# Batch 0's keys and queries projected twice side by side and written in place by the engines, batch 1 prepared between the first heads

## The chip, the cores and the metric

One Trainium2 chip, one of its cores. The metric is the device time of one execution in microseconds (us). The kernel before took 519.92, 517.23 and 517.09 us in three runs; the median is 517.23 us.

TensorE (PE) multiplies, VectorE (DVE) and ScalarE (ACT) read its results out of PSUM, GpSimd (POOL) works on SBUF alone, and SyncE (SP) issues the DMAs. Each runs its own list of instructions in order and waits on semaphores.

## The reference, cut to what matters

Two layers over x (4 batches of 256 tokens, width 128) and a context (4 batches of 512 rows, width 96). The change touches the attention of layer 0; what follows it is only told in words.

```python
B, S, _ = x.shape            # after a layer norm of x;  4, 256
scale = DIM_HEAD ** (-0.5)   # 8 heads of 64
q = (x @ Wq).reshape(B, S, HEADS, DIM_HEAD).transpose(0, 2, 1, 3)
k = (context @ Wk).reshape(B, L, HEADS, DIM_HEAD).transpose(0, 2, 1, 3)
v = (context @ Wv).reshape(B, L, HEADS, DIM_HEAD).transpose(0, 2, 1, 3)
attn = jnp.einsum('bhsd,bhld->bhsl', q, k) * scale
attn = jax.nn.softmax(attn, axis=-1)
out = jnp.einsum('bhsl,bhld->bhsd', attn, v)
return out @ Wo + bo
```

Then come layer 0's feed-forward part (fixed-point rounding and a piecewise linear GELU), layer 1's attention (16 heads of 8), a small feed-forward part and a mixture of 8 experts, two per token.

## The kernel before, in words

Everything runs from one list of steps, `order`, that `schedule()` builds: each step has a kind and indices, as ("k0", 1, 3), and each engine walks the list and does its part of every step that it knows. So the list sets the order of work on every engine. Iteration `it` of the list is one batch of one layer (0 to 3 layer 0, 4 to 7 layer 1); a step stands at a place counted in heads of that iteration, from the table PLACES, or from SHIFTED where that names the iteration. Iteration it computes scores and outputs of its batch and, between the heads, prepares the next.

Layer 0 keeps keys and queries as 16-bit high and low parts, so that a score is a sum of products over a stacked axis. For a head, kA holds the high part of the key twice (64 rows each), qA the high part of the query over its low part, kB the low part of the key, qB the high part of the query; rows 64 to 67 of kB and qB carry a selector and the row maxima, which a score subtracts. Projections, transposes and maxima all pass through four PSUM banks, the ring p_misc. For a projection TensorE takes a bank (`misc_take`), ScalarE writes the high part, and VectorE writes the difference, which frees it.

- `keys0` ("k0", b, m): two heads at once, 128 rows (L423); ScalarE copies to kx (L1004), VectorE takes the difference (L748). `queries0` ("q0", b, i): likewise (L447, L1023, L753), into qx.
- `stack0` ("stack0", b): kx and qx have two heads over each other and must be sorted into kA, kB, qA and qB. SyncE does so with 12 DMAs (L1247 to L1249), six for the keys once all four key steps are done, then six for the queries.
- `maxima` ("max", 0, b, h): scores of tokens by keys for the row maxima (L464, reduced at L759); for h = 0 it waits for all 12 DMAs. `rows`: the maxima of four heads are transposed and copied into qB (L773).
- `scores` ("sc", 0, b, h): L491, then the exponential on ScalarE (L1042). GpSimd sums each head's four tiles ("sum", L1181 to L1183), and `attend` ("av", L510) multiplies with the values; its fourth chunk ends with the sums' product (L517), which waits for GpSimd, and the sums of the next four heads wait for it.
- `init`: memsets on VectorE (L764, L765) and GpSimd; ("init", 4) is a block on GpSimd that prepares layer 1's kS (L1155 to L1165). "ln", "xn", "xT": layer norm; its square root comes from GpSimd (L1139, L1140), in GpSimd's order.

Of the kernel before, what the change touches and what calls it, by code (L numbers as in the profile page):

```python
# [5 lines left out]
ALU = mybir.AluOpType  # L6
# [5 lines left out]
P = 128  # L12
# [23 lines left out]
    0: {"max": (1.5, 1.0), "sum": 1.38, "av": (-0.38, 0.96), "f_ln": -0.65, "f_xn": 0.92, "f_xT": 1.2,  # L36
        "up0": (1.4, 0.13), "round": 1.57, "floor": 2.0, "nodes": 2.17, "slope": 3.0, "interp": 3.5, "ident": 3.7,
# [3 lines left out]
        "zeros": 3.67, "init": (1.0, 2.0), "rows": 0.84},  # L41
    1: {"max": (2.4, 1.01), "av": (0.3, 1.0), "f_ln": 0.18, "f_xn": 1.29, "f_xT": 1.39, "up0": (1.87, 0.4),
        "round": 2.76, "floor": 2.8, "nodes": 3.39, "slope": 4.4, "interp": 5.2, "ident": 5.69, "down0": 5.86,
        "q1_ln": 8.4, "q1_xn": 9.17, "q1_xT": 10.0, "q1": 11, "k1": 9.53, "bounce": 11.61, "sT": 4.1,
        "oT": (4.64, 2.0), "aT": (6.0, 2.0), "y0": (7.3, 2.0), "oT1": (4.52, 0.7), "aT1": 6.54, "h1": 8.28,
        "y1": 9.07, "v1": 5.94, "stage": (0.62, 1.9), "split": (0.6, 1.9), "ex_ln": (11.14, 1.0),
        "ex_xn": (12.57, 1.0), "ex_xT": (12.68, 1.0), "logits": (14.14, 1.0), "route": 16.14, "rows": 2.43},
# [17 lines left out]
def schedule():  # L65
# [18 lines left out]
    for what in first:  # L84
        put(-1, 0, *what)
    for n, h in enumerate(range(4, H0)):
        put(0, 0.5 + 0.6 * n, "max", 0, 0, h)
    put(0, 3.1, "rows", 0, 0, 1)
    put(0, 0.1, "k0", 1, 3)
    for i in range(2):  # L90
        put(0, 0.7 + 0.6 * i, "q0", 1, i)
# [1252 lines left out]
```

## Time and profile before

| what | us |
|---|---|
| median of three runs (all: 517.09, 517.23, 519.92) | 517.23 |
| span of the profiled execution (its own time outside the span isn't given) | 515.0 |
| TensorE busy in the span | 440.4 |
| VectorE busy | 367.9 |
| ScalarE busy | 266.9 |
| GpSimd busy | 175.6 |

The span begins with the first instruction that the profiler records, and the times of all views are counted from there. A busy TensorE is one with a matmul in flight; at which of its two clocks it ran is told by the granted clock, 1.00 for 2.4 GHz and 0.50 for 1.2 GHz. In front of an instruction stands how long its engine had been idle, and what ended that; "issue" means that the profile shows nothing it waited for, which is how a wait for a DMA can look.

### The profile page before, as it was taken

The page shows a single profiled execution, that of the slowest core. Times are in us where ns is not written, and L with a number is a line of the kernel's source. Part 1 is how long each engine was busy: PE and PEld are TensorE (multiplying, and loading weights), DVE is VectorE, ACT ScalarE, POOL GpSimd, SP SyncE. Part 2 cuts the span into 40 slices and gives each one's busy share as a digit, 9 for nine tenths or more (in the row PEclk, how much of TensorE's full clock was granted, in tenths as well). Part 3 has the DMA queues.
Part 4 walks back from the last instruction along what each step waited for, and adds up shares of the span by engine and source line. Part 5 has one row for each costly group of instructions (what it writes and reads, how often), then busy time and mean ns, then how long its engine had stood idle before and what let it go on. Part 6 is the DMA issues. An engine that isn't in the chain of part 4 may idle for free.

```text
span 515.0 us, 8942 instructions
## 1 busy us (share of the span) xinstructions
PE 440.4 (86%) x3344; PEld 250.5 (49%) x3344; DVE 367.9 (71%) x718; ACT 266.9 (52%) x504; POOL 175.6 (34%) x205
## 2 busy tenths in 40 slices
PE   8569698995779868969975995999989999999996
PEld 4225354563356445535432542544536665656565
DVE  5665374654875798879958994794368787987875
ACT  4415244642725632475656363668765555554653
POOL 4307954634554572750516041630130004000000
PEclk9867798997899988997997898999999999999999
DMA  5755316017004006331262027210000000000000
GB/s 160 170 122 116 67 28 158 1 27 158 22 1 57 1 1 154 57 91 33 73 84 84 2 73 87 83 42 2 2 1 1 1 2 0 2 22 2 1 1 22
DMA packets 33023, 25.91 MB, mean 50 GB/s; under 512 B 4589, under 2 KB 30381, under 8 KB 32877
## 3 DMA queue, kind: packets, MB, share of 16 engines
q1 hardware_dynamic: 32981, 25.35, 22.2%
q8 instruction: 27, 0.44, 0.4%
q14 instruction: 15, 0.12, 0.1%
HBM read 12.10 MB, written 2.10 MB: 28 GB/s over the span
## 4 chain that ended last, share of the span: by engine, by line
PE 57%; DVE 22%; ACT 7%; issue 7%; DMA 3%; SPq 2%; POOL 1%; DVEq 0%; POOLq 0%; ACTq 0%
PE p_o L663 7%; PE p_misc L646 7%; PE p_sc L491 6%; PE p_sc L646 6%; DVE mx L759 6%; PE p_misc L464 6%; PE p_o L523 4%; PE p_o L510 4%; PE p_misc L397 4%; DVE xn L722 3%; PE p_misc L423 3%; DVE probs L946 2%; DMA region<-kx 2%; PE p_misc L555 2%; ACT probs L1108 2%
## 5 line engine op out<-in xcount | busy, mean ns | idle before, releaser
L759 DVE TENSOR_REDUCE mx<-p_misc 128x1 f32<-128x512 f32 x192 | 122.4, 684 | 41.9 <-PE p_misc L464 40.3
L1042 ACT ACTIVATE probs<-p_sc 128x512 f32<-128x512 f32 x192 | 104.5, 596 | 65.9 <-PE p_sc L491 65.6
L1108 ACT ACTIVATE probs<-p_misc 128x512 f32<-128x512 f32 x64 | 38.1, 597 | 56.6 <-PE p_sc L646 56.6
L946 DVE TENSOR_TENSOR probs<-probs,p_sc 128x512 f32<-128x512 f32 x64 | 44.0, 687 | 26.5 <-ACT probs L1108 24.6
L464 PE MATMUL p_misc<-kS,qS 96*128 96x512 f16 x128 | 41.9, 404 | 16.7 <-issue 8.5
L646 PE MATMUL p_misc<-qS,region 128*128 128x512 f16 x192 | 52.1, 380 | 3.8 <-DVE probs L946 2.6
L646 PE MATMUL p_sc<-qS,region 128*128 128x512 f16 x192 | 51.9, 379 | 0.0
L1181 POOL TENSOR_TENSOR psums<-probs 128x256 f32<-128x256 f32 x32 | 26.0, 811 | 61.5 <-PE p_o L517 58.0
L663 PEld LDWEIGHTS p_o<-region,probs 128*128 128x128 f16 x720 | 42.7, 98 | 7.1
L663 PE MATMUL p_o<-region,probs 128*128 128x128 f16 x720 | 45.1, 219 | 0.0
L1139 POOL TENSOR_SCALAR veps<-meanvar 128x2 f32<-128x2 f32 x16 | 3.5, 218 | 121.7 <-DVE meanvar L711 121.2
L491 PE MATMUL p_sc<-qS,kS 128*128 128x256 f16 x256 | 41.3, 282 | 4.1 <-ACT probs L1042 3.8
L510 PE MATMUL p_o<-probs,v 128*64 128x256 f32 x256 | 38.2, 423 | 7.1 <-ACT probs L1042 7.1
L951 DVE TENSOR_TENSOR probs<-probs 128x512 f16<-128x512 f32 x64 | 43.8, 684 | 0.0
L523 PE MATMUL p_o<-probs,v 128*32 128x256 f32 x512 | 41.5, 402 | 0.0
L1115 ACT CAST probs<-probs 128x512 f16<-128x512 f32 x64 | 39.1, 611 | 1.4 <-DVE probs L946 1.4
L491 PE MATMUL p_sc<-region 128*128 128x256 f16 x256 | 35.8, 286 | 0.9 <-DVE region L773 0.9
L491 PEld LDWEIGHTS p_sc<-qS,kS 128*128 128x128 f16 x256 | 23.6, 99 | 19.8 <-ACT probs L1042 7.9
L464 PE MATMUL p_misc<-region 128*128 128x512 f16 x64 | 22.0, 426 | 12.7 <-issue 12.5
L491 PEld LDWEIGHTS p_sc<-region 128*128 128x128 f16 x256 | 25.5, 102 | 12.3 <-issue 3.7
L1199 POOL TENSOR_TENSOR region<-v,region 128x512 f16<-128x512 f32 x24 | 29.3, 1222 | 1.9
L646 PEld LDWEIGHTS p_sc<-qS,region 128*128 128x128 f16 x192 | 18.8, 98 | 22.6
(163 smaller groups left out, 678.5 us busy)
## 6 DMA issues: line engine op xcount, KB each, us to landing
region<-kx SPq DMA_DIRECT2D x24, 256.0 KB
v<-in_L_ffn_W_dram SPq DMA_DIRECT2D x24, 256.0 KB, 2.8
region<-qx SPq DMA_DIRECT2D x24, 128.0 KB
kS<-kS SPq DMA_DIRECT2D x1, 1664.0 KB
kS<-k_scratch SPq DMA_DIRECT2D x12, 128.0 KB
k_scratch<-kx SPq DMA_DIRECT2D x4, 256.0 KB, 3.1
qS<-q_scratch SPq DMA_DIRECT2D x12, 64.0 KB
probs<-in_ctx_dram SPq DMA_DIRECT2D x1, 576.0 KB, 6.0
```

What stands on the lines that cost most here:

```text
L464: pe.matmul(ps, q[:, i * P:(i + 1) * P], k, start=True, stop=True).then_inc(full, 1)
L491: last = pe.matmul(p_sc[:, half, j * S:(j + 1) * S], k[:, kt * P:(kt + 1) * P], q, start=(i == 0), stop=(i == len(pairs) - 1))
L510: pe.matmul(p_o[64 * i:64 * i + 64, 0, m * S:(m + 1) * S], v0[:, b % 2, kt, h * DH0:(h + 1) * DH0], probs[:, h % 8, kt * S:(kt + 1) * S], ...
L523: last = pe.matmul(p_o[32 * j:32 * j + 32, n % 2, 0:S], v1[:, b % 2, c, h * VW:h * VW + 32], probs[:, h % 8, c * S:(c + 1) * S], start=(c ...
L646: last = pe.matmul(ps[:, f % 2, :], w[:, ws, e, f * P:(f + 1) * P], xh[:, xs, half * C:(half + 1) * C], start=(i == 0), stop=(i == 2))
L663: last = pe.matmul(p_o[:, n % 2, i * P:(i + 1) * P], hh[:, n % 2, hs, f, i * P:(i + 1) * P], ew[2][:, ws, e, f * P:(f + 1) * P], start=(at ...
L759: dve.tensor_reduce(mx[:, b % 2, i, h:h + 1], ps, AX_X, ALU.max).then_inc(free, 1)
L946: dve.tensor_tensor(hp[:, k % 2, :], sg[:, k % 2, :], p_sc[:, k % 2, :], ALU.mult).then_inc(hp_done, 1)
L951: dve.tensor_tensor(hh[:, n % 2, 1, f, :], hp[:, k % 2, :], hh[:, n % 2, 0, f, :], ALU.subtract).then_inc(hl_done, 1)
L1042: act.activation(probs[:, h % 8, half * 512:(half + 1) * 512], p_sc[:, half, :], ACT.Exp, scale=(DH0 if layer == 0 else DH1) ** -0.5).then ...
L1108: act.activation(sg[:, k % 2, :], p_misc[:, k % 2, :], ACT.Silu).then_inc(sg_done, 1)
L1115: act.copy(hh[:, last_n % 2, 0, last_f, :], hp[:, (k - 1) % 2, :]).then_inc(hh_done, 1)
```

## The change

Batch 0 no longer passes through kx, qx and DMAs. `keys0_twice` projects one head into both halves of the 128 output rows, as two matmuls of 64 columns of weights side by side; ScalarE writes both halves straight into kA, VectorE writes the difference into kB. `queries0_twice` does the same for two heads: ScalarE writes the high part twice into qA, VectorE replaces the lower half by the difference, and GpSimd copies the upper half into qB. So batch 0 has eight key steps and four query steps in place of four and two. The product over kB and qB now reads 68 rows instead of 128, so only four rows of kB are zeroed and none of qB. Batch 0's twelve DMAs go. The first list ends after four heads' maxima; what remained of batch 0 and all of batch 1's preparation (context, values, keys, queries, norms) stand between the first heads of iteration 0. The 15 loads of later weights stand before the DMAs of batch 1. All places were chosen anew, those of the later iterations too.

```diff
-    0: {"max": (1.5, 1.0), "sum": 1.38, "av": (-0.38, 0.96), "f_ln": -0.65, "f_xn": 0.92, "f_xT": 1.2,
...
+    0: {"max": (1.5, 1.0), "sum": 1.38, "av": (-0.38, 0.96), "f_ln": -1.31, "f_xn": 0.76, "f_xT": 1.2,
...
 SHIFTED = {
...
-    first = [("init", 0), ("warm", 10), ("ln", "q0", 0), ("split_w", 0), ("cT", 0), ("warm", 6), ("xn", "q0", 0), ("k0", 0, 0), ("warm", 4), ("xT", "q0", 0), ("k0", 0, 1), ("k0", 0, 2), ("k0", 0, 3),
-             ("q0", 0, 0), ("q0", 0, 1), ("stack0", 0), ("split_w", 1), ("cT", 1), ("ln", "q0", 1), ("v0", 0, 0), ("v0", 0, 1), ("xn", "q0", 1), ("init", 1),
-             ("v0", 0, 2), ("v0", 0, 3), ("cT", 2), ("cT", 3), ("xT", "q0", 1),
-             ("max", 0, 0, 0), ("k0", 1, 0), ("max", 0, 0, 1), ("k0", 1, 1), ("max", 0, 0, 2), ("k0", 1, 2), ("max", 0, 0, 3), ("rows", 0, 0, 0)]
+    first = [("zero", 0), ("warm", 10), ("ln", "q0", 0), ("split_w", 0), ("cT", 0), ("warm", 6), ("init", 0), ("xn", "q0", 0), ("k0h", 0), ("xT", "q0", 0), ("k0h", 1),
+             ("q0h", 0), ("k0h", 2), ("max", 0, 0, 0), ("k0h", 3), ("q0h", 1), ("max", 0, 0, 1), ("max", 0, 0, 2), ("k0h", 4), ("max", 0, 0, 3), ("k0h", 5), ("q0h", 2), ("rows", 0, 0, 0)]
...
+            put(it, place["q0b"][0] + place["q0b"][1] + 0.01 if it == 0 else -0.01, "stack0" if nxt[0] == 0 else "stack1", nxt[1])
...
+            def keys0_twice(h):
+
+                if h == 0:
+                    pe.wait_ge(wc_split, 1)
+                    misc_done(pe, ("cT", 0))
+                ps, full = misc_take(pe, ("k0h", h))
+                for i, (ws, cs) in enumerate(((0, 0), (1, 0), (0, 1))):
+                    for rows in (slice(0, DH0), slice(DH0, P)):
+                        last = pe.matmul(ps[rows, :], wc[:, ws, h * DH0:(h + 1) * DH0], cT[:, cs, 0:C], start=(i == 0), stop=(i == 2))
+                last.then_inc(full, 1)
+
+            def queries0_twice(i):
...
+                ps, full = misc_take(pe, ("q0h", i))
+                for j in range(2):
+                    h = 2 * i + j
+                    for rows in (slice(0, DH0), slice(DH0, P)):
+                        last = pe.matmul(ps[rows, j * S:(j + 1) * S], wq0[:, h * DH0:(h + 1) * DH0], xT[:, 0, :], start=True, stop=True)
+                last.then_inc(full, 1)
...
+                if layer == b == 0:
+                    pe.wait_ge(k_first, h + 1)
+                    misc_done(pe, ("q0h", h // 2))
...
-                    pairs = [(kA[:, b % 2, h, :], qA[:, b % 2, h, :]), (kB[:, b % 2, h, :], qB[:, b % 2, h, :])]
+                    if b == 0:
+                        misc_done(pe, ("k0h", h))
+                        pe.wait_ge(q_second, h // 2 + 1)
+                    pairs = [(kA[:, b % 2, h, :], qA[:, b % 2, h, :]), (kB[0:SEL0 + 4, b % 2, h, :], qB[0:SEL0 + 4, b % 2, h, :])]
...
+            def keys0_twice(h):
+                dve.wait_ge(k_first, h + 1)
+                ps, free = misc_wait(dve, ("k0h", h))
+                dve.tensor_tensor(kB[0:DH0, 0, h, :], ps[0:DH0, :], kA[0:DH0, 0, h, :], ALU.subtract).then_inc(free, 1)
...
-                if b and m == 0:
-                    act.wait_ge(k_stacked, 96 * b)
+                if b >= 2 and m == 0:
+                    act.wait_ge(k_stacked, 96 * (b - 1))
...
+                act.copy(kA[:, 0, h, :], ps).then_inc(k_first, 1)
...
+                pool.tensor_copy(qB[0:DH0, 0, high, :].rearrange("p h n -> p (h n)"),
+                                 qA[0:DH0, 0, high, :].rearrange("p h n -> p (h n)")).then_inc(q_second, 1)
```

**TensorE, the first projections up to batch 0's first maxima.** L423 is the key projection, L447 the queries, L431 the values, L397 transposes (of context rows where they read probs, of tokens where they read xn), L464 the maxima; in the changed kernel L488 and L499 are the doubled projections, L453 the transposes and L541 the maxima. Before:

```order
L423 MATMUL p_misc<-cT,wc 128x512 x3
L414 MATMUL p_o<-qx 128x512 x4
L397 MATMUL p_misc<-ident,xn 128x128 x2
L423 MATMUL p_misc<-cT,wc 128x512 x9
L447 MATMUL p_misc<-xT,wq 128x256 x4
L397 MATMUL p_misc<-ident,probs 96x128 x4
L431 MATMUL p_misc<-wc,cT 128x512 x12
L397 MATMUL p_misc<-ident,probs 96x128 x8
L397 MATMUL p_misc<-ident,xn 128x128 x2
L464 MATMUL p_misc<-region 128x512 x2
```

And in the changed kernel:

```order
L488 MATMUL p_misc<-cT,wc 64x512 x6
L453 MATMUL p_misc<-ident,xn 128x128 x2
L488 MATMUL p_misc<-cT,wc 64x512 x6
L499 MATMUL p_misc<-xT,wq 64x256 x4
L488 MATMUL p_misc<-cT,wc 64x512 x6
L541 MATMUL p_misc<-region 128x512 x2
L488 MATMUL p_misc<-cT,wc 64x512 x6
L499 MATMUL p_misc<-xT,wq 64x256 x4
L541 MATMUL p_misc<-region 128x512 x4
```

The first maxima stand behind three doubled key steps and one query step, and the values and the other context transposes have moved behind them.

**TensorE, from batch 1's last projections (where its DMAs are issued) to its first maxima.** L491 and L571 are the scores, L510 and L590 the products with the values, L477 and L521 the single projections in the changed kernel; the last row of each piece is ("max", 0, 1, 0), which waits for the DMAs. Before:

```order
L447 MATMUL p_misc<-xT,wq 128x256 x2
L464 MATMUL p_misc<-region 128x512 x2
L491 MATMUL p_sc<-region 128x256 x8
L464 MATMUL p_misc<-region 128x512 x2
L491 MATMUL p_sc<-region 128x256 x8
L397 MATMUL p_misc<-ident,mx 4x128 x2
L423 MATMUL p_misc<-cT,wc 128x512 x3
L510 MATMUL p_o<-probs,v 64x256 x4
L464 MATMUL p_misc<-region 128x512 x2
```

And in the changed kernel:

```order
L521 MATMUL p_misc<-xT,wq 128x256 x2
L571 MATMUL p_sc<-region 128x256 x8
L541 MATMUL p_misc<-region 128x512 x2
L477 MATMUL p_misc<-cT,wc 128x512 x6
L571 MATMUL p_sc<-region 128x256 x8
L453 MATMUL p_misc<-ident,mx 4x128 x2
L477 MATMUL p_misc<-cT,wc 128x512 x6
L590 MATMUL p_o<-probs,v 64x256 x4
L541 MATMUL p_misc<-region 128x512 x2
```

All four key steps of batch 2 now stand ahead of batch 1's first maxima, where one did.

**GpSimd, the block for kS among batch 0's sums.** L1181 to L1183 and L1285 to L1287 are one head's sum, L1158 to L1162 with the four selections L1145 (in the changed kernel L1255 to L1259 and L1242) are the block, L1236 and L1237 are ("ln", "q0", 3). Before, from the fourth head's sum:

```order
L1181 TENSOR_TENSOR psums<-probs 128x256
L1182 TENSOR_TENSOR psums<-psums,probs 128x256
L1183 TENSOR_TENSOR psums<-psums,probs 128x256
L1158 MEMSET tri 128x64
L1159 AFFINE_SELECT tri<-tri 128x64
L1162 MEMSET kS 128x4096
L1145 AFFINE_SELECT kS<-kS 32x2048 x4
L1181 TENSOR_TENSOR psums<-probs 128x256
```

In the changed kernel, from the sixth head's sum:

```order
L1285 TENSOR_TENSOR psums<-probs 128x256
L1286 TENSOR_TENSOR psums<-psums,probs 128x256
L1287 TENSOR_TENSOR psums<-psums,probs 128x256
L1255 MEMSET tri 128x64
L1256 AFFINE_SELECT tri<-tri 128x64
L1259 MEMSET kS 128x4096
L1242 AFFINE_SELECT kS<-kS 32x2048 x4
L1285 TENSOR_TENSOR psums<-probs 128x256
L1286 TENSOR_TENSOR psums<-psums,probs 128x256
L1287 TENSOR_TENSOR psums<-psums,probs 128x256
L1236 TENSOR_SCALAR veps<-meanvar 128x2
L1237 TENSOR_TENSOR rstd<-veps,mhalf 128x2
```

The block has moved behind two more sums: from ahead of the fifth head's sum to between the sixth's and the seventh's, and ahead of batch 3's norm.

## Rows read from the trace of the kernel before

**Rows 1.** The page's first part: busy us, share of the span, instructions.

```profile
PE 440.4 (86%) x3344; PEld 250.5 (49%) x3344; DVE 367.9 (71%) x718; ACT 266.9 (52%) x504; POOL 175.6 (34%) x205
```

**Rows 2.** TensorE's waits: us in total, times, longest.

```profile
PE p_misc L464 <- issue: 21.0, 5, 6.2
```

**Rows 3.** The chain of waits: start us, us, what.

```profile
52.87 3.68 issue
```

**Rows 4.** Groups of instructions, VectorE, 0 to 57 us: busy us, mean ns, idle.

```profile
L759 DVE TENSOR_REDUCE mx<-p_misc 128x1 f32<-128x512 f32 x16 | 10.2, 682 | 4.2 <-PE p_misc L464 4.2
L748 DVE TENSOR_TENSOR kx<-p_misc,kx 128x512 f16<-128x512 f32 x9 | 6.1, 691 | 8.1 <-ACT kx L1004 8.1
L764 DVE MEMSET region<- 64x2048 f32 x2 | 3.5, 1765 | 1.0 <-issue 1.0
```

**Rows 5.** Timeline to 40 us: start us, us, engine, line; in brackets the idle before.

```profile
8.03 0.81 PE L423 MATMUL p_misc<-cT,wc 96*128 96x512 f16 x3 [0.17 <-DVE cT L743]
...
13.55 0.73 SPq L1247 DMA_DIRECT2D region<-kx  x1
...
16.23 4.45 PE L431 MATMUL p_misc<-wc,cT 96*128 96x512 f16 x12 [1.96 <-DVE wc L737]
...
27.53 1.01 PE L464 MATMUL p_misc<-region 128*128 128x512 f16 x2 [5.75 <-issue]
...
38.08 1.89 PE L491 MATMUL p_sc<-region 128*128 128x256 f16 x8 [0.91 <-DVE region L773]
```

**Rows 6.** Windows, 18 to 20 us: busy by engine, granted clock, DMA.

```profile
18.00:20.00 2.00, 2.00 (x6) 0.68 (x5) 0.77 (x3) 0.71 (x2) 0.64 (x1) 0.50 0.91 210
```

**Rows 7.** Timeline, 42 to 57 us: batch 1's DMAs, batch 2's first key copy, the maxima.

```profile
42.74 0.60 SPq L1247 DMA_DIRECT2D region<-kx  x1
...
52.89 0.58 ACT L1004 CAST kx<-p_misc 128x512 f16<-128x512 f32 x1 [2.08 <-DMA region<-kx]
...
56.55 1.01 PE L464 MATMUL p_misc<-region 128*128 128x512 f16 x2 [4.53 <-issue]
```

**Rows 8.** Timeline, TensorE, 74 to 77 us: products side by side between whole ones.

```profile
74.37 0.81 PE L431 MATMUL p_misc<-wc,cT 96*128 96x512 f16 x3
75.11 1.08 PE L510 MATMUL p_o<-probs,v 128*64 128x256 f32 x8
76.13 0.60 PE L464 MATMUL p_misc<-region 128*128 128x512 f16 x2
```

**Rows 9.** Timeline, 55 to 84 us: GpSimd's block, sums and norm, and who follows.

```profile
55.68 3.51 POOL L1162 MEMSET kS<- 128x4096 f32 x1
...
59.34 8.14 POOL L1145 TENSOR_SCALAR_AFFINE_SELECT kS<-kS 32x2048 f16<-32x2048 f16 x4
...
72.37 0.73 POOL L1181 TENSOR_TENSOR psums<-probs 128x256 f32<-128x256 f32 x1 [4.90 <-PE p_o L517]
...
79.92 0.71 POOL L1140 TENSOR_TENSOR rstd<-veps,mhalf 128x2 f32<-128x2 f32 x1
...
81.75 1.43 DVE L722 TENSOR_SCALAR xn<-x_sb,meanvar,rstd 128x128 f32<-128x128 f32 x2
...
83.24 0.44 PE L397 MATMUL p_misc<-ident,xn 128*128 128x128 f32 x2 [1.21 <-DVE xn L722]
```

**Rows 10.** Timeline, 112 to 130 us: batch 3's DMAs, its first maxima, a feed-forward product.

```profile
112.78 0.59 SPq L1247 DMA_DIRECT2D region<-kx  x1
...
126.59 1.01 PE L464 MATMUL p_misc<-region 128*128 128x512 f16 x2 [2.24 <-issue]
...
127.39 1.91 PE L555 MATMUL p_misc<-xT,f0w 128*128 128x256 f32 x4
```

**Rows 11.** Timeline, TensorE, three later waits for maxima of layer 1.

```profile
228.86 0.39 PE L464 MATMUL p_misc<-kS,qS 96*128 96x512 f16 x1 [2.10 <-DVE rden L778]
...
270.06 0.59 PE L464 MATMUL p_misc<-kS,qS 96*128 96x512 f16 x2 [2.23 <-issue]
...
277.98 0.61 PE L464 MATMUL p_misc<-kS,qS 96*128 96x512 f16 x1 [4.24 <-DVE mx L759]
```

More of the change, by code:

```diff
@@ new lines @@
+    (2, 'f_ln'): -0.22, (2, 'floor'): 2.08, (2, 'init'): (1.75, 1.58), (2, 'initb'): 1.47, (2, 'interp'): 3.48,
+    (2, 'k0b'): (2.05, 0.4), (2, 'k0h'): (0.36, 0.4), (2, 'lnb'): -1.95, (2, 'max0'): (0.32, 0.78),
+    (2, 'q0'): (2.15, 0.82), (2, 'q0_ln'): 0.21, (2, 'q0b'): (1.9, 0.38), (2, 'q1'): 5.66, (2, 'q1_ln'): 4.48,
+    (2, 'round'): 1.68, (2, 'rows'): 1.95, (2, 'slope'): 2.73, (2, 'sum'): 2.36, (2, 'v0'): (3.6, 1.02),
+    (2, 'v0a'): (0.56, 0.25), (2, 'v1'): 5.51, (2, 'xTb'): 0.97, (2, 'xnb'): 0.36, (2, 'zeros'): 3.55,
@@ L681, in down_last @@
                     last.then_inc(y_full, 1)
-            steps = {"dn_last": down_last, "warm": warm, "cT": context, "k0": keys0, "v0": values0, "xT": xt, "q0": queries0, "max": maxima, "rows": rows, "sc": scores,
+            steps = {"dn_last": down_last, "warm": warm, "cT": context, "k0": keys0, "k0h": keys0_twice, "q0h": queries0_twice, "v0": values0, "xT": xt, "q0": queries0, "max": maxima, "rows": rows, "sc": scores,
                      "av": attend, "sT": sums_t, "oT": heads_t, "aT": heads_back, "y0": project0, "up0": up0, "down0": down0,
@@ L974, in _ @@
             dve.memset(warm_in.bitcast(F32), 0.0).then_inc(warm_set, 1)
-            steps = {"split_w": split_w, "cT": context, "ln": norm, "xn": normed, "xT": xt, "k0": keys0, "q0": queries0, "init": init, "max": maxima, "rows": rows, "sT": sums_t, "oT": heads_t,
+            steps = {"split_w": split_w, "cT": context, "ln": norm, "xn": normed, "xT": xt, "k0": keys0, "k0h": keys0_twice, "q0h": queries0_twice, "q0": queries0, "zero": zero, "max": maxima, "rows": rows, "sT": sums_t, "oT": heads_t,
                      "y0": project0, "round": rounded, "floor": floor, "slope": slope, "interp": interp, "ident": identity, "down0": add0,
@@ L1115, in activate @@
                     act.copy(hh[:, last_n % 2, 0, last_f, :], hp[:, (k - 1) % 2, :]).then_inc(hh_done, 1)
-            steps = {"split_w": split_w, "cT": context, "k0": keys0, "v0": values0, "xT": xt, "q0": queries0, "rows": rows, "sc": softmax, "av": outputs,
+            steps = {"split_w": split_w, "cT": context, "k0": keys0, "k0h": keys0_twice, "q0h": queries0_twice, "v0": values0, "xT": xt, "q0": queries0, "rows": rows, "sc": softmax, "av": outputs,
                      "aT": heads_back, "up0": up0, "nodes": nodes_at, "k1": keys1, "q1": queries1, "aT1": heads_back1, "h1": up1,
@@ L1211, in _ @@
             pool.sem_inc(const_pe, 1)
-            steps = {"ln": norm, "sum": sums, "init": init, "route": route, "split": split}
+            steps = {"ln": norm, "q0h": queries0_twice, "sum": sums, "init": init, "route": route, "split": split}
             for kind, *at in order:
```

132 lines of the change are left out of this document (89 added, 43 removed), and 32 rows, old and new, of tables (PLACES, SHIFTED).

## The prediction

> **What bounds the kernel now.** The page's first part comes first: TensorE is busy 440.4 of 515.0 us, VectorE 367.9 [rows 1]. No engine is full, so the question is where TensorE stands still. Its waits answer: five times it stood at maxima with nothing in the profile to wait for, 21.0 us in all [rows 2]. These are the first maxima of a batch, and what they wait for are DMAs: the first needed 13.98 us from the first DMA (13.55) to the maxima (27.53), with TensorE idle for 5.75 [rows 5], the second 13.81 (42.74 to 56.55) with 4.53 idle [rows 7], and the chain of waits has that wait on the path [rows 3]. After each such stop TensorE works at half clock: two maxima take 1.01 us at 56.55 [rows 7] and 0.60 at 76.13 [rows 8]. The change takes away the first of these stops and rearranges what surrounds the second. The reader should see that the first score stands at 38.08 [rows 5], but that batch 1's maxima, 18.5 us later, are the next gate, and that they hang on when batch 1's DMAs begin, not on when batch 0 begins.
>
> All times below are of the profiled execution (span 515.0); the median of the runs, 517.23, lies 2.2 above it, and I subtract my sum from the median.
>
> **Step 1, batch 0's first score.** The doubled key step starts where the single one does, 8.03 [rows 5]. Two products side by side cost little more than one: the block at 75.11 holds eight 64-column halves, and the next instruction starts 1.02 later [rows 8], where one after the other they would take 1.7. So I take 0.75 for a doubled key step (a single one 0.64, 0.81 with its tail) and 1.0 for a doubled query step. Following the steps through TensorE, ScalarE (0.58 a copy) and VectorE (0.69), the first doubled query is done at 12.65 and the fourth pair of maxima at 21.1; the maxima's transpose, its two copies and the waits between bring the first score to 23, 15 us earlier than before.
>
> **Step 2, the start of batch 1's DMAs.** They need the last of batch 1's key steps. What VectorE must do from 12.65 until then, by the list: 6 doubled keys, 3 doubled queries, 4 keys and 1 query, 3 context parts, all at 0.69 (17 of them, 11.7), 7 pairs of maxima at 1.28 (eight took 10.2; 9.0), one memset of 1.76 [rows 4], and 3.5 of small ones, an estimate. That is 25.9, so 38.5 if it never waits. My walk has it wait 1.7 more, where a doubled query or a softmax pair stands ahead of it on ScalarE: **40.3**. Before, it was 42.74 [rows 7]. Here the gain of step 1 goes: batch 0's preparation was overlapped with DMA waits, and now values, contexts and batch 1's keys follow after the first score. The zeroing of qB (one memset of about half L764's time per batch) is gone, and four more keys and two more queries cost VectorE 4.1; both are in the count. Bounds: 38.5, and 50 if TensorE ran at half clock throughout (its work in this stretch is some 25 us at full clock).
>
> **Step 3, batch 1's first maxima.** The keys land 10.15 after the first DMA (52.89 less 42.74), and ScalarE's copy of batch 2's first key waits for just that [rows 7]. In the new order this copy stands in front of the fourth head's softmax, and the fourth key step and the first value products in front of the maxima. So: 40.3 + 10.15, two copies, a softmax pair of 1.1 (as two copies), then value products at half clock, 2.0: the maxima start at 55.1, not 56.55. The queries' DMAs have landed by 54.1 and no longer end the wait. Three key steps of batch 2 are behind us that were ahead before.
>
> **Step 4, GpSimd's block.** From here TensorE needs some 7.9 us to the sums' product of the first four heads (three chunks of values, two scores, three maxima pairs, part of it at half clock): 63.0, where before it ended at 72.17, 0.2 before the sum at 72.37 that waited for it [rows 9]. GpSimd's order now decides. Three heads' sums and the norm's root take 8.26 (72.37 to 80.63); before, they were all that followed. Now the block for kS stands among them, 3.51 + 8.14 [rows 9] and an estimated 0.45 for the small triangle ahead of them, 12.1. The root is ready at 63.0 + 0.2 + 8.26 + 12.1 = 83.6, the normalised tokens 1.43 later, and TensorE's transpose of batch 3's tokens starts at **85.1**, before it was 83.24 [rows 9]. TensorE would be there at about 78, so some 7 us of the lead are waited away: +1.9 in place of a gain. Behind it one value step (1.29 at half clock, twice its 0.64) is already done, and value products now cover the copy of the transposed tokens (an estimated 0.46): +0.2 is left.
>
> **Step 5, batch 3.** Its DMAs start after the last score of batch 1, and 13.81 later the maxima follow (112.78 to 126.59) [rows 10]. One value step moves behind that score: -0.65. Two steps that stood behind the maxima, a product of the feed-forward part at 1.91 [rows 10] and the transposed maxima, now fall into the wait: -1.9 for TensorE; VectorE's rounding, which ends the next chain, gains less, and I take -1.0.
>
> **Step 6, the later places.** A maxima pair now stands before batch 3's reciprocals on VectorE, and another before the slope; these two waits of TensorE were 2.10 and 4.24 [rows 11]. I take half of them, 3.2, since the work put behind is due as well. Against it one feed-forward product moves out of the wait at 270.06 [rows 11]: +1.0. Together -2.2; bounds -6.3 (both waits gone) and +2.2 (neither, and something else late).
>
> **At nothing:** the 15 weight loads, which now run before 20 us (nobody waits for them before layer 0's output); GpSimd's four copies of query halves (it is idle there; if they took 2 us each they would still be ahead of the first scores); the narrower product over 68 rows; the first clearing of kB. The layer 1 reordering from 325 us on: neither side is worth a sign.
>
> **Sum:** +0.2 - 0.65 - 1.0 - 2.2 = -3.65, so 517.23 - 3.65 = **513.6**.
>
> **A rule of the skill against the trace.** The value products side by side start at 75.11, before the full-width ones in front of them have ended (75.18), and the full-width ones behind start at 76.13, before their end (76.19) [rows 8]: no time is lost at the change of shape. The Trainium skill (TensorEngine Tiling (Array Packing), Tiling Modes, Key Properties) says that changing the tiling mode drains TensorE. The trace speaks against that as a cost here. By that rule the head would have some 18 changes at 0.17, half of them on the path, and the sum would be 515.1, an estimate.
>
> **The rivals.**
> - *The lead is kept (0.18).* GpSimd's block does not stand in the way, because the sums' product comes earlier than I have it or the tokens are needed later. The lead at that product is 9.2, less 2.9 for the six steps now behind it; 6.3 less some waiting at batch 2's maxima, 6, takes the place of +0.2: 517.2 - 6 - 0.65 - 1.0 - 2.2 = 507.4. For it: the order is new everywhere. Against: the block's place between two sums is plain in the list.
> - *Slower: TensorE's clock falls in the head (0.14).* After 1.96 us without work the granted clock went to 0.50 [rows 5, 6]. From 12 to 40 us TensorE is now busy three quarters, in pieces of 0.4 to 1.0 with gaps up to 1.3. At half clock the doubled steps take 1.5 and 2.0 and TensorE sets the pace instead of VectorE. The place is the stretch before batch 1's DMAs; each us of delay there goes on to the end. If they start at 46.5 rather than 40.3 and step 6 gives nothing: 517.2 + 6.4 - 0.65 - 0.5 = 522.5. It decides from a start at 44 on, where the other gains are used up.
> - *Not side by side (0.07).* If the halves ran one after the other, or each change of shape drained the array (0.17, the tail of 0.81 over 0.64 at 8.03, at 18 changes: 3.1), TensorE would have 3 to 7 us more in the head, half of it on the path: about 517.
> - *The late places give nothing (0.20).* 515.8 to 517.5.
> - *The forecast (0.41)*, 511 to 516; I give 0.19 of it to below 512.1.
>
> **The numbers.** Predicted 513.6. The range takes in the first rival and, of the slower one, all but its end: 506 to 521.5. One per cent, 5.2 us, is about what a measurement of this kernel can tell from no change: faster by more than that 0.18 + 0.19 = 0.37, slower 0.15 (the second rival and a little of the others), within 0.48.
>
> **What the new profile would show.** Step 1: the first score near 23. Step 2: first DMA from kx near 40, with VectorE almost gapless before it; a start after 44 with a granted clock of 0.50 is the slower rival. Step 3: batch 1's first maxima near 55, behind value products. Step 4: POOL's kS memset starting near 68, and TensorE idle some 7 us at a transpose of tokens near 85; if that idle time is missing, the first rival holds. Step 5: a feed-forward product inside the wait before batch 3's maxima. Step 6: the waits of 2.10 and 4.24 halved. I am wrong if the head's 15 us arrive at batch 2's scores at all, or if a new wait stands in layer 1, where I have looked at order only.

## The result

| | before | changed |
|---|---|---|
| median of the runs, us | 517.27 (4 runs, 517.09 to 519.92) | 526.21 (4 runs, 525.68 to 526.77) |
| ratio, 95% interval | | 1.0146 [1.011, 1.0181] |
| the same, measured again (the last experiment) | 519.02 (11 runs) | 526.24 (6 runs), 1.0122 [1.0078, 1.0166] |
| profiled execution, span | 515.0 | 524.2 (its time 526.16) |
| mean granted TensorE clock | 0.934 | 0.922 |

The change makes the kernel 7 to 9 us slower. The forecast was 513.6 with a range of 506 to 521.5, and 0.15 for slower.

On the page of the changed kernel TensorE answers to [rows 1] with 11.2 us more of busy time, for 56 matmuls more. The four windows further down hold 11.2 us of it with nearly the same count of matmuls, so there it works slower, not more.

```profile
PE 451.6 (86%) x3400; PEld 256.1 (49%) x3400; DVE 373.5 (71%) x722; ACT 269.4 (51%) x510; POOL 178.9 (34%) x209
```

TensorE's waits (us in total, times, longest) answer to [rows 2]. The waits of the maxima for DMAs ("issue") fell from 21.0 to 7.7. Two single waits took their place: 7.8 for VectorE's part of a key of batch 2, which itself waits for a DMA, and 8.0 for normalised tokens.

```profile
PE p_misc L453 <- DVE xn L802: 16.0, 7, 8.0
PE p_misc L477 <- DVE kx L828: 7.8, 1, 7.8
PE p_misc L541 <- issue: 7.7, 3, 5.5
```

**The head.** The timeline of the changed kernel, against [rows 5, 7] (start us, us, engine, line; in brackets the idle time before): a doubled key step, the first score, the first DMA of batch 1, ScalarE's copies of batch 2's keys, which wait for it, batch 2's last key step, batch 1's first maxima, and the first four heads' sums' product.

```profile
7.98 0.84 PE L488 MATMUL p_misc<-cT,wc 96*64 96x512 f16 x6 [0.38 <-DVE cT L823]
...
23.79 0.39 PE L571 MATMUL p_sc<-region 128*128 128x256 f16 x2
...
40.73 0.73 SPq L1351 DMA_DIRECT2D region<-kx  x1
...
50.95 1.07 ACT L1093 CAST kx<-p_misc 128x512 f16<-128x512 f32 x2 [9.18 <-DMA region<-kx]
...
52.31 1.46 PE L477 MATMUL p_misc<-cT,wc 96*128 96x512 f16 x3 [7.77 <-DVE kx L828]
...
55.61 1.03 PE L541 MATMUL p_misc<-region 128*128 128x512 f16 x2
...
63.20 0.64 PE L597 MATMUL p_o<-psums,ones 128*32 128x256 f32 x8
```

The first score is 14.3 us earlier, the DMAs 2.0, the maxima 0.9. The product is 8.3 earlier (it started at 71.5 in the kernel before). Then comes GpSimd, against [rows 9]: its block for kS, the root for batch 3's tokens, the tokens on VectorE, and TensorE's transpose.

```profile
69.51 3.51 POOL L1259 MEMSET kS<- 128x4096 f32 x1
...
73.17 8.08 POOL L1242 TENSOR_SCALAR_AFFINE_SELECT kS<-kS 32x2048 f16<-32x2048 f16 x4
...
84.20 0.71 POOL L1237 TENSOR_TENSOR rstd<-veps,mhalf 128x2 f32<-128x2 f32 x1
...
85.01 1.59 DVE L802 TENSOR_SCALAR xn<-x_sb,meanvar,rstd 128x128 f32<-128x128 f32 x2 [5.54 <-POOL rstd L1237]
...
86.65 0.69 PE L453 MATMUL p_misc<-ident,xn 128*128 128x128 f32 x2 [7.96 <-DVE xn L802]
```

The whole lead is gone here: the sums' product of the second four heads (the second group) starts at 93.6, before it was 92.4.

**Behind the head** 1.2 us of lateness become 8.9 by 366 us (the same transpose of tokens stands at 366.8 and at 375.7), and stay. Windows between the same products of both kernels (stretch, length, then busy time by engine, and third from last the granted clock), first before:

```profile
133.60:159.70 26.10, 19.68 (x141) 12.44 (x143) 20.48 (x34) 12.53 (x21) 13.46 (x14) 0.93 0.08 21
159.70:205.70 46.00, 38.01 (x260) 23.16 (x258) 36.96 (x66) 21.19 (x38) 25.60 (x31) 0.93 0.28 53
205.70:251.30 45.60, 38.98 (x290) 22.42 (x288) 39.34 (x72) 25.17 (x47) 22.66 (x29) 0.93 0.24 57
251.30:301.80 50.50, 39.07 (x301) 19.89 (x300) 41.57 (x74) 28.50 (x56) 17.61 (x20) 0.90 0.28 57
```

and the changed kernel:

```profile
134.90:164.10 29.20, 22.48 (x139) 14.73 (x138) 19.12 (x32) 12.79 (x21) 13.44 (x14) 0.82 0.06 19
164.10:211.00 46.90, 40.52 (x260) 24.81 (x258) 38.26 (x67) 20.94 (x38) 26.06 (x31) 0.85 0.26 52
211.00:258.40 47.40, 40.18 (x299) 23.00 (x298) 41.04 (x73) 26.05 (x49) 22.98 (x28) 0.93 0.20 51
258.40:311.50 53.10, 43.76 (x300) 22.29 (x300) 42.31 (x75) 28.99 (x57) 17.42 (x20) 0.84 0.27 60
```

The four together are 8.4 us longer. In three of them (6.6 of the 8.4) TensorE's busy time grew by 2.5 to 4.7 us with nearly the same count of matmuls, and the granted clock fell from 0.93 or 0.90 to 0.82 to 0.85. In the third window, 1.8 us longer, the clock is the same, and a wait of 2.10 us has become 3.46 (shown further down).

### The profile page after: what moved, and what is told of

It reads as the page before. It is cut to its first block, busy times and chain, and to the rows that moved or that the text cites. A ratio compares the mean times of both kernels' runs of the same rounds, so it can differ in the third digit from the quotient of the medians.

```text
span 524.2 us, 9069 instructions
## 1 busy us (share of the span) xinstructions
PE 451.6 (86%) x3400; PEld 256.1 (49%) x3400; DVE 373.5 (71%) x722; ACT 269.4 (51%) x510; POOL 178.9 (34%) x209
## 4 chain that ended last, share of the span: by engine, by line
PE 58%; DVE 21%; ACT 5%; issue 5%; POOL 5%; DMA 3%; SPq 1%; POOLq 0%; DVEq 0%; ACTq 0%
PE p_o L743 7%; PE p_sc L571 7%; PE p_misc L726 6%; PE p_sc L726 6%; PE p_misc L541 6%; PE p_o L590 5%; PE p_o L603 5%; DVE mx L851 4%; PE p_misc L453 4%; PE p_misc L645 2%; DVE xn L802 2%; DVE probs L1035 2%; PE p_misc L635 2%; ACT probs L1205 2%; POOL kS L1242 1%
## 5 line engine op out<-in xcount | busy, mean ns | idle before, releaser
L541 PE MATMUL p_misc<-kS,qS 96*128 96x512 f16 x128 | 42.6, 410 | 16.8 <-DVE mx L851 7.7
L1285 POOL TENSOR_TENSOR psums<-probs 128x256 f32<-128x256 f32 x32 | 25.7, 803 | 63.6 <-PE p_o L597 57.1
L590 PE MATMUL p_o<-probs,v 128*64 128x256 f32 x256 | 39.7, 437 | 6.7 <-ACT probs L1139 6.7
L571 PE MATMUL p_sc<-qS,kS 128*128 128x256 f16 x256 | 42.7, 288 | 1.4 <-ACT probs L1139 0.9
L1236 POOL TENSOR_SCALAR veps<-meanvar 128x2 f32<-128x2 f32 x16 | 4.0, 249 | 114.8 <-DVE meanvar L791 114.6
L571 PE MATMUL p_sc<-region 128*128 128x256 f16 (+1 forms) x256 | 36.2, 286 | 0.0
L571 PEld LDWEIGHTS p_sc<-qS,kS 128*128 128x128 f16 x256 | 23.6, 103 | 20.2 <-issue 7.0
L571 PEld LDWEIGHTS p_sc<-region 128*128 128x128 f16 (+1 forms) x256 | 25.9, 103 | 11.5 <-issue 3.1
L1302 POOL CAST region<-v 128x512 f16<-128x512 f32 x24 | 16.6, 691 | 42.0 <-DMA v<-in_L_ffn_W_dram 41.4
```

The lines of the kernel that those rows point to most:

```text
L541: pe.matmul(ps, q[:, i * P:(i + 1) * P], k, start=True, stop=True).then_inc(full, 1)
L571: last = pe.matmul(p_sc[:, half, j * S:(j + 1) * S], k[:, kt * P:(kt + 1) * P], q, start=(i == 0), stop=(i == len(pairs) - 1))
L590: pe.matmul(p_o[64 * i:64 * i + 64, 0, m * S:(m + 1) * S], v0[:, b % 2, kt, h * DH0:(h + 1) * DH0], probs[:, h % 8, kt * S:(kt + 1) * S], ...
```

## The experiments

All ratios are to the kernel before, run beside them on the same chip, with 95% intervals. One execution of a kernel differs from the next by up to 0.9% either way in these runs, so a difference below some 0.5% between two experiments is not resolved.

**Which part costs?** Two theories: the later places cost the time themselves (A), or the head does (B). Four runs. In the first, the entries of the two tables of places for iterations 2 to 7 are those of the kernel before, for instance

```diff
-    (3, 'k1'): -0.05, (3, 'sT'): 4.74, (4, 'y1'): 6.03, ...
+    (3, 'k1'): 2.03, (3, 'sT'): 3.68, (4, 'y1'): 9.07, ...
```

> The changed kernel, with the places of the kernel before for the third to eighth batch (iterations 2 to 7); the doubled projections, the first list and the places of iterations 0 and 1 stay as changed. Theory A (the later places cost the time, 8 us by the table of starts: the second group's sums' product is only 1.2 us late at 93.6, everything after that is growth): 517 to 519 us, the first query transpose still 3 us late with its wait of 8 us. Theory B (the head's lateness sets in what phase the later batches run, and the clock falls with it, whatever the later places are): 524 to 527 us.

Measured: 1.0034 [0.9998, 1.007], 520.57 us. That lies in neither range, nearer to A: 0.9% (4.6 us) of the second measurement of the changed kernel, 1.0122, are gone. The wait of 8.0 us at 87 is still there.

The second moves GpSimd's kS block (and with it, by one sum, a clearing of qS of 1.80 us; every other engine's list stays):

```diff
-    (0, 'init'): (2.99, 1.87),
+    (0, 'init'): (2.99, 1.22),
```

> The changed kernel with one edit: GpSimd's clearing and filling of kS (12.6 us) stands before the sums of heads 4 and 5 instead of behind them, so that it runs where GpSimd idles from 57.4 to 64.1 us. Both theories: the wait of 8 us for the normalised queries at 86.65 goes, since the block ends near 70 and the rstd is computed near 76 and no longer at 84.2; the second group's sums' product starts near 86 and no longer at 93.6. Theory A: that lead is kept in part, 518 to 523 us, the growth of the later batches stays. Theory B: the growth goes with it, 512 to 517 us. If the lead is lost at the next transfer instead, 525 to 527 us.

Measured: 0.9953 [0.9922, 0.9983], 515.88 us. Its trace, where the block begins in GpSimd's idle time (it ends some 4 us after the next sum could have begun) and the root comes 7.7 us earlier:

```profile
56.93 3.51 POOL L1259 MEMSET kS<- 128x4096 f32 x1
60.58 8.08 POOL L1242 TENSOR_SCALAR_AFFINE_SELECT kS<-kS 32x2048 f16<-32x2048 f16 x4
...
76.49 0.71 POOL L1237 TENSOR_TENSOR rstd<-veps,mhalf 128x2 f32<-128x2 f32 x1
...
80.66 0.44 PE L453 MATMUL p_misc<-ident,xn 128*128 128x128 f32 x2 [0.71 <-DVE xn L802]
```

The second group's product starts at 86.7, 6.9 us earlier than in the changed kernel, and the two traces are 7 to 10 us apart everywhere behind it. One number in a table takes 1.7% (8.8 us) off, and makes the change faster than the kernel before. The time is in B's range, but the other half of B, that the growth behind the head goes with its lateness, is not what the trace shows: the four windows take 29.1, 46.9, 47.4 and 52.2 us at clocks of 0.82, 0.85, 0.93 and 0.84, as in the changed kernel, and the lead over the kernel before, 5.7 us at this product, is used up by the end of the span (515.7 against 515.0; the profiled execution was the slowest of its 12).

The third is the kernel before with the changed later places:

> The kernel before, with the changed kernel's places for iterations 2 to 7 and nothing else of the change. Theory A (the later places cost the time themselves): 522 to 526 us. Theory B: 516 to 518.5 us.

Measured: 1.0009 [0.9976, 1.0042], 519.29 us, just above B's range. A falls in its plain form: beside the old head no cost of these places is resolved.

The fourth is the first one for iterations 4 to 7 alone, and a fifth, sent later, does iterations 2 and 3 alone:

> The changed kernel with the places of the kernel before for iterations 4 to 7 alone. In the changed kernel the lateness is 5.3 us by 205 us and 9 us by 366 us. Theory A: the share of the places from iteration 4 on, some 3.5 us, goes: 521.5 to 523.5 us. Theory B: 524 to 527 us.

> The changed kernel with the places of the kernel before for iterations 2 and 3 alone. With those of 4 to 7 it was 1.0126 of the kernel before, with all of 2 to 7 1.0034, and as it stands 1.0122. If the loss of the later places lies in iterations 2 and 3 (the order around down0, where the clock stays low longer): 1.003 to 1.006, 521 to 522 us. If each half alone does nothing and only both together do: 1.010 to 1.014.

Measured: 1.0126 [1.0074, 1.0178], 524.96 us, and 1.0097 [1.0061, 1.0133], 523.43 us. Neither half gives back what both do (1.0034).

The traces tell more of the later places than the times do. Us from the second sums' product to the fourth (that of 133.6 before and 134.9 changed), and from the fourth to the end:

| trace | second to fourth | fourth to end |
|---|---|---|
| kernel before | 41.2 | 381.4 |
| the same with the changed later places | 38.9 | 385.9 |
| changed kernel | 41.4 | 389.3 |
| the same with the old later places | 42.5 | 381.9 |
| changed kernel, block early | 40.1 | 389.0 |
| the same with the old later places (below) | 43.2 | 385.0 |

Beside each of the three heads the changed later places give 1.1 to 3.2 us in the first stretch and take 4.0 to 7.4 in the second. Each row is one execution, comparable to 2 or 3 us only (last section), so the signs are better shown than the sizes.

**The block's place by itself.** The kernel before, with GpSimd's block where the change has it. Two clearings of qS (1.80 us each) move by two sums with it; the lists of all other engines do the same work in the same order:

```diff
-    (0, 'init'): (0.81, 2.0),
+    (0, 'init'): (2.99, 1.87),
```

> The kernel before with GpSimd's kS block at the changed kernel's place, behind the sums of heads 4 and 5, and nothing else; every other engine's list is the same. If the block's place is what costs the changed kernel its time: the block starts near 77 and ends near 90 and no longer at 67.5, the query transpose of 83.2 waits for it until near 94, and the time is 525 to 529 us. If it matters only beside the new head or later places: 517 to 520 us.

Measured: 1.0209 [1.0172, 1.0246], 529.97 us, 1 us above the first case. The transpose of [rows 9], which waited 1.21 us at 83.24:

```profile
93.07 0.69 PE L397 MATMUL p_misc<-ident,xn 128*128 128x128 f32 x2 [12.88 <-DVE xn L722]
```

This edit alone makes the kernel before slower than the changed one.

**Only the root behind the block?** The changed kernel, its block where it was, with batch 3's statistics and root ahead of it:

```diff
-            step("q0_ln", "ln", "q0", b + 2)
+            put(0, 4.3, "ln", "q0", 3) if it == 1 else step("q0_ln", "ln", "q0", b + 2)
```

> The changed kernel with this one edit: the statistics and rstd of batch 3's queries ahead of the sums of head 3; the kS block stays behind the sums of heads 4 and 5. If what costs the time is only the rstd that queues behind the block on GpSimd: the wait of 8.0 us at 86.7 goes though the block stands where it did, and the time is that of the block moved early, 515 to 519 us. If the block costs it otherwise too (the sums of heads 6 and 7 behind it, which the product at 93.6 reads, end at 88.9): 519 to 522 us.

Measured: 0.9985 [0.9945, 1.0026], 519.39 us, some 1.4% less than the changed kernel and at the lower end of the second case. The wait is halved, not gone. GpSimd's select, VectorE's copy of maxima and tokens, and the transpose:

```profile
73.44 8.09 POOL L1242 TENSOR_SCALAR_AFFINE_SELECT kS<-kS 32x2048 f16<-32x2048 f16 x4
```

```profile
77.60 2.15 DVE L862 COPY region<-mrow 4x1024 f16<-4x1024 f16 x1 [1.08 <-ACT mrow L1077]
79.79 2.07 DVE L802 TENSOR_SCALAR xn<-x_sb,meanvar,rstd 128x128 f32<-128x128 f32 x2
```

```profile
81.92 0.69 PE L453 MATMUL p_misc<-ident,xn 128*128 128x128 f32 x2 [3.91 <-DVE xn L802]
```

The root is no longer late. VectorE's two instructions are slow beside the select: 2.15 and 2.07 us, where the kernel before needs 0.72 and 1.43 beside GpSimd's sums, so the block costs some 2 us of the 3.91 a second time (the last section has more).

**Both edits together**, block early and old later places:

> Both earlier edits in one kernel: the changed kernel with GpSimd's kS block before the sums of heads 4 and 5, and the places of the kernel before for iterations 2 to 7. If the two costs are separate (the wait of 8 us in the head; slower TensorE stretches of the later places), they add: the run with the block alone gave 0.9953 of the kernel before and the run with the old later places took 1.1% off the changed kernel, so about 0.984 to 0.988, 510 to 512 us. If the later stages give back any lead of the head (the last transfers and waits bind), it stays at 515 to 518 us.

Measured: 0.9916 [0.988, 0.9953], 515.67 us, the second case. That is less than the sum: a part of the lead is given back. By the traces it is 6.7 us at the second group's product (85.7 against 92.4), 4.7 at 129, and 1 to 2 from 250 us on: the stretch around the feed-forward product takes 27.4 us against 26.1, and a wait of 2.1 at 229 has become 3.25 at 228. The places, 0.9% beside the changed head, are 0.4% here, which the intervals don't separate from none.

**One exchange on TensorE.** In iteration 2 the change puts four transposes of sums ahead of a score. Soon behind them comes the feed-forward product (`down0` in the expectations, its 16 matmuls read f0w and kS), and "the stretch" is the first of the four windows, from the sums' product ahead of it to the next. The same exchange made back, in the kernel with the block early, and made alone in the kernel before:

```diff
 L510 MATMUL p_o<-probs,v 64x256 x4
-L491 MATMUL p_sc<-region 128x256 x8
 L397 MATMUL p_misc<-ident,ssb 128x128 x4
+L491 MATMUL p_sc<-region 128x256 x8
 L565 MATMUL p_misc<-f0w,kS 128x128 x8
```

> The kernel with the block early and one exchange on PE in iteration 2: the four transposes of the sums (sT of batch 1) stand behind the scores of head 4 again, as in the kernel before; every engine's list is otherwise the same. Theory C (this exchange alone makes the clock fall later and lets it stay low over down0): the stretch between the sums' products around down0, 29.1 us now, is 26 us as in the kernel before, and down0's first 16 matmuls take 2.05 us and not 3.42; in all 511.5 to 514 us. Theory D (the clock's fall there is made by the whole set of later places): the stretch stays at 28.5 to 29.5 us and the time at 515 to 517 us.

> The kernel before with that one exchange made in it: the transposes of the sums ahead of the scores of head 4 in iteration 2, nothing else. Theory C: its stretch of 26.1 us around down0 becomes 29 us and the time 519.5 to 521.5 us, about 1.005 of the kernel before. Theory D: the stretch stays within 0.5 us of 26.1 and the time within 1 us.

TensorE in the kernel before, and then in the kernel with only this exchange:

```profile
139.92 1.98 PE L510 MATMUL p_o<-probs,v 128*64 128x256 f32 x8 [3.51 <-ACT probs L1042]
141.83 1.60 PE L491 MATMUL p_sc<-region 128*128 128x256 f16 x8
143.26 0.60 PE L397 MATMUL p_misc<-ident,ssb 128*128 128x128 f32 x4
144.92 2.05 PE L565 MATMUL p_misc<-f0w,kS 128*128 128x128 f32 x16 [1.06 <-DVE kS L832]
```

```profile
140.57 1.08 PE L510 MATMUL p_o<-probs,v 128*64 128x256 f32 x8 [3.59 <-ACT probs L1042]
141.58 0.95 PE L397 MATMUL p_misc<-ident,ssb 128*128 128x128 f32 x4
142.33 1.91 PE L491 MATMUL p_sc<-region 128*128 128x256 f16 x8
145.57 3.50 PE L565 MATMUL p_misc<-f0w,kS 128*128 128x128 f32 x16 [1.32 <-DVE kS L832]
```

Both stand idle 3.5 us for ScalarE and 1.1 to 1.3 for VectorE. In the first the clock is already low when TensorE resumes (1.98 for the value products, 1.08 at full speed) and is back before the feed-forward product (2.05). In the second the products run at full speed, the clock falls behind them, VectorE's wait lies inside the slow stretch, and the product takes 3.50.

The stretch was 29.1 us in the kernel before with the exchange, as theory C had it, and 27.7, not 26, with the exchange made back. But the value products stand ahead of the exchanged steps, and up to them the two lists shown are the same. So the exchange did not decide whether they met the low clock, and these two traces alone don't show what it does. All sixteen traces of this study do better:

| value products at the wait of 3.5 us | transposes ahead: length of the stretch | transposes behind |
|---|---|---|
| 1.08 to 1.14 us, clock still high | 29.1 to 29.4 (6 traces) | 27.4 to 27.8 (3) |
| 1.49 to 1.98 us, clock low in them | 27.8 (1) | 26.0 (3), 27.7 (3) |

Where the clock falls behind the value products, the transposes ahead go with a stretch some 1.6 us longer. Where it falls ahead of them the stretch is shorter by up to as much again, and what decides that stays open. The times show neither: 0.9982 [0.9948, 1.0016], 518.11 us, for the kernel before with the exchange, where C had 1.005, and 0.9923 [0.9888, 0.9957], 515.45 us, for the one without (0.9953 with it), where C had 511.5 to 514. An effect on the time is not shown.

**Can the lead be kept?** Three more steps on top of both edits. First TensorE's idle time before batch 1's DMAs land is filled:

```diff
-    (0, 'k0'): (2.56, 0.35), (0, 'v0'): (7.37, 0.37),
+    (0, 'k0'): (3.63, 0.05), (0, 'v0'): (2.5, 0.01),
```

> The kernel with both edits (block early, old later places), and in iteration 0 the work moved into TensorE's idle time before batch 1's transfer lands (7.9 us at 53): batch 1's four value steps ahead of it, batch 2's key steps behind the first outputs, so that ScalarE no longer waits for the transfer ahead of the exponentials of head 3. If the lead of the head reaches the end: 4 to 6 us less than the run with both edits, 506 to 508 us. If the transfer of batch 2, for which TensorE already waits 1.1 us at 85, takes it: within 1.5 us of that run.

Measured: 0.9883 [0.9839, 0.9926], 513.29 us, between the two cases: 2.4 less than the run with both edits and not separated from it. TensorE still stops for the same DMAs, now with nothing in between:

```profile
54.31 1.01 PE L541 MATMUL p_misc<-region 128*128 128x512 f16 x2 [5.57 <-DMA region<-qx]
```

Then batch 1's projections stand ahead of batch 0's values. Cut to the line that does most of it; three entries beside it (k0h, q0h, initb) bring batch 0's last key and query steps and batch 1's clearing forward too:

```diff
-        "cTb": (-0.13, 0.3), "lnb": -0.5, "xnb": 0.0, "xTb": 0.68, "k0b": (0.7, 0.4), "q0b": (1.8, 0.1),
+        "cTb": (-0.13, 0.3), "lnb": -0.5, "xnb": 0.0, "xTb": 0.05, "k0b": (0.06, 0.01), "q0b": (0.1, 0.01),
```

> The kernel of the filled idle time, with batch 1's query transpose, key and query steps moved behind the scores of head 0, ahead of batch 0's values, and so its transfers. If those transfers are what binds the head (they start at 40.7 us, their wait ends at 55.6, TensorE idles 5.6 us for them even with the idle time filled): they start near 33 and land near 48, TensorE's wait at 54 goes, and 3 to 6 us go with it, 507 to 511 us. If the next transfers (batch 2's, waited for at 83 and 120) take it: within 1.5 us of the run with the filled idle time.

Measured: 0.9861 [0.9812, 0.991], 511.35 us, 1.9 less and again not separated. The first DMA starts at 33.4, the wait at 54 is gone, the first sums' product stands at 56.3 (63.3 without). But TensorE then waits 6.1 us for tokens at 76.0: the root stands behind the kS block again, and 1.5 of the 7 us reach the second product. So the last step takes it out from behind, with the line shown above for the root:

> The run with batch 1 first, and the statistics and rstd of batch 3's queries moved ahead of the sums of head 3 and of the kS block, behind which GpSimd computes it at 73.5 us there (TensorE waits 6.1 us for it at 76.0). The wait goes, the transposes start near 70 and the second group's sums' product, 83.4 there, near 77; if that lead holds, 505 to 508 us; if batch 2's transfers take it (their wait of 0 there comes back as 4 to 6 us near 77), within 1.5 us of the run before it, 511.4.

Measured: **0.9791 [0.9743, 0.9838], 508.46 us**, the fastest of all and 2% faster than the kernel before, half a us above the first case. At the second product its trace leads the kernel before by 12.8 us, at the end by 8.0: here too a part of the lead is given back. Its DMAs, the transpose, batch 2's first maxima without a wait, and the second group's product:

```profile
33.35 0.73 SPq L1351 DMA_DIRECT2D region<-kx  x1
```

```profile
71.90 0.69 PE L453 MATMUL p_misc<-ident,xn 128*128 128x128 f32 x2 [1.62 <-DVE xn L802]
...
78.00 0.66 PE L541 MATMUL p_misc<-region 128*128 128x512 f16 x2
...
79.60 0.64 PE L597 MATMUL p_o<-psums,ones 128*32 128x256 f32 x8
```

The changed kernel itself, again:

> The changed kernel itself, to have its time beside the other runs on one chip: 1.012 to 1.018 of the kernel before, some 525 to 527 us.

Measured: 1.0122 [1.0078, 1.0166], 526.24 us.

## Why the prediction was wrong

**Steps 1 to 3 held.** First score at 23.79 (forecast 23), first DMA at 40.73 (40.3), batch 1's first maxima at 55.61 (55.1), behind value products and with ScalarE's copy waiting for the keys. A doubled key step takes 0.84 against 0.81 for a single one [rows 5], its halves of 64 columns side by side, so the rival of halves one after the other is out. VectorE was busy 26.0 of the 28.1 us from 12.65 to 40.73, at a granted clock of 1.00, so the rival of a falling clock in the head is out too. Step 3 owes a part of its hit to luck: its terms add up to 54.7, not 55.1, and not the softmax pair (1.1) stood between the copies and the value products but batch 2's last key step at half clock, 1.39.

**The reading on the change of shape was wrong.** The prediction took overlapping records in [rows 8] for proof that no time is lost when TensorE goes from full-width products to halves side by side. An end in a record can lie behind the next start, so what counts is the distance between starts. In the changed kernel:

```profile
11.45 1.03 PE L499 MATMUL p_misc<-xT,wq 128*64 128x256 f32 x8
12.32 0.82 PE L488 MATMUL p_misc<-cT,wc 96*64 96x512 f16 x6
...
15.14 1.03 PE L499 MATMUL p_misc<-xT,wq 128*64 128x256 f32 x8
16.11 0.60 PE L541 MATMUL p_misc<-region 128*128 128x512 f16 x2
```

The same eight halves are followed after 0.87 us by more halves, and after 0.97 by full-width products. [rows 8] has it as well: three value projections take 0.74 to the halves at 75.11. The last section has the number over the whole trace, 0.09 to 0.10 a change. The Trainium skill (TensorEngine Tiling (Array Packing), Tiling Modes, Key Properties) says that changing the tiling mode drains TensorE, and the trace agrees. Up to the second group's product the change has 33 such changes where there were 17, so some 1.5 us more of TensorE's time in the head, put at nothing in the sum; as VectorE sets the pace there to 40 us, only a part can be on the path.

**Step 4 held in its mechanism and was cut off too early.** Forecast: root ready at 83.6, transpose at 85.1, some 7 us of lead waited away, +0.2 left. The trace: ready at 84.9, 86.65 after a wait of 7.96, and +1.2 at the second group's product. The run with old later places, 1.0034, ends 1.8 us late by its median, with an interval that just reaches no change. The wait was also the largest single item: moving the block gives 8.8 us in the changed kernel, and 10.9 the other way in the kernel before. The prediction had it as a gain that fails to come; the price of its first rival, 6.2 below the forecast, was the right kind of number and somewhat small.

**Step 5 held in half.** Batch 3's first maxima start at 128.70 with 0.73 idle before, and the feed-forward product is ahead of them. From the maxima (2.1 late, 126.59 before) to the product at 134.9 (1.3 late) the lateness falls by 0.8; forecast was 1.0. But batch 3's DMAs start at 114.98, 2.2 us late, where the second product was 1.2 late: 1.0 lost and not 0.65 gained. Together 0.15 us was lost from 93.6 to 134.9, where the forecast had a gain of 1.65.

**Step 6 failed; its sign was wrong.** Forecast: -2.2, bounds -6.3 to +2.2. Measured: from the product at 134.9 to the end the trace loses 7.9 us, and putting the old places back takes 4.6 us off the time (1.0122 to 1.0034; by the intervals 2 to 7). The changed kernel's later waits, against [rows 11]:

```profile
236.57 0.39 PE L541 MATMUL p_misc<-kS,qS 96*128 96x512 f16 x1 [3.46 <-DVE mx L851]
...
276.24 1.01 PE L541 MATMUL p_misc<-kS,qS 96*128 96x512 f16 x2 [1.48 <-issue]
...
285.64 0.46 PE L541 MATMUL p_misc<-kS,qS 96*128 96x512 f16 x1 [1.93 <-DVE mx L851]
...
295.31 0.39 PE L541 MATMUL p_misc<-kS,qS 96*128 96x512 f16 x1 [1.89 <-DVE a L960]
```

The wait of 4.24 was halved as forecast, the one of 2.10 grew (it is 3.18 with the old later places too, so these places did not bring it), and a new one of 1.89 stands at 295. But waits are not where most of the time went: the windows show it as busy time at a lower clock. I had priced these places as waits moved about, each stretch at the clock it had before, so that neither the forecast nor the upper bound held a change of the clock behind the head.

What stays open is why the same places cost 0.9% beside this head with its late block, 0.4% (not resolved) with the block early, and nothing that is resolved beside the old head. By the table above a part of the answer is that they give back 1 to 3 us ahead of the fourth product. The traces of these places beside the old head and beside the changed one agree in the stretch around the feed-forward product (29.5 and 29.2 us, clock 0.83 and 0.82) and part behind it:

```profile
160.50:205.60 45.10, 37.66 (x261) 22.71 (x259) 38.21 (x67) 20.95 (x38) 26.10 (x31) 0.92 0.27 54
252.40:303.70 51.30, 40.76 (x300) 20.42 (x299) 43.20 (x74) 28.58 (x56) 17.55 (x20) 0.90 0.28 62
```

against 46.90 at 0.85 and 53.10 at 0.84 in the changed kernel, for the same lists. How long the clock stays low thus depends on more than the order of the steps. That the slow clock goes with these places is seen in the traces; that it is what joins head and places is argued, not shown.

## What to carry to other kernels

When a change brings an engine's work forward, look on the engines beside it for a long piece of work that nobody waits for, and for what small result is queued behind it: here 12 us of clearing with a root of 0.7 us behind it turned a head that was 6 us faster into one that was 1 us later than before. A wait that only eats a gain should be priced as a loss to be removed, since the edit that removes it may be one number. And where the clock falls after waits, an order of steps has no fixed price: give later reorderings a bound on the slow side that holds the stretch at half clock.

## What the runs showed of the hardware

**VectorE beside GpSimd's select.** The ten instructions that normalise tokens in the changed kernel up to 123 us, of one form (ns, shortest, median, longest):

```profile
L802 DVE TENSOR_SCALAR xn<-x_sb,meanvar,rstd x10: 331/704/1944, 8.2 to 122.7; 128x128 f32<-128x128 f32 x10
```

Alone one takes 0.33 to 0.34; the four beside GpSimd's sums of two tensors (85.0 and 122.0) take 0.79 or 0.88. The longest is the one that meets a select, at 8.26:

```profile
8.15 2.21 DVE L802 TENSOR_SCALAR xn<-x_sb,meanvar,rstd 128x128 f32<-128x128 f32 x2 [0.31 <-POOL rstd L1237]
```

```profile
8.26 4.06 POOL L1242 TENSOR_SCALAR_AFFINE_SELECT region<-region 4x2048 f16<-4x2048 f16 x2
```

With the root ahead of the block it happens again: 2.07 for two beside the selects, and 2.15 for a copy of maxima that takes 0.42 alone. With the block early the pair meets the clearing of kS instead (3.51 us from 56.93) and takes 2.38 from 58.20, until 0.1 us after the clearing ends. VectorE's reductions out of PSUM and its subtractions out of PSUM beside the same selects keep their 0.68 and 0.69. The Trainium skill (SBUF — State Buffer, Terms) says that VectorE and GpSimd share a pair of ports that is locked for a whole instruction, and that the loser is fully blocked. The trace agrees: one select lasts 2.02 us (8.08 for four), the longest delay, 1.61 over the 0.33, is within one, and the instruction ends 0.1 us after the select.

**TensorE at a change of width.** By the starts of single matmuls in the two traces, at full clock: a product with 512 columns of moving data is followed after 0.215 us by one of the same width of weights, and after 0.306 to 0.309 where the next works on 64 or 32 columns of weights side by side; with 256 columns it is 0.109 and 0.202; from halves back to full width 0.317 in place of 0.215, and from halves to quarters 0.315. So each change costs 0.09 to 0.10 us, in either direction. The kernel before has 192 of them, the changed one 210.

**Executions of one kernel.** The kernel before ran between 515.1 and 523.6 us over four sets of 11 to 29 runs. The stretch around the feed-forward product comes in three lengths over the sixteen traces, near 26, 27.6 and 29.2 us, and where the granted clock falls and returns differs with them. That makes single traces of this kernel comparable to 2 or 3 us only.
